# Splits of VectorE to GpSimd and ScalarE, five pair tiles ahead of the exchanged tiles and three behind, and x2 added per quarter

## The chip, the cores and the metric

The kernel runs on one core of a Trainium2 chip. The metric is the time of one execution on the device in microseconds (us). The core has five engines that run side by side, each with its own order of instructions: TensorE (PE, matrix products; PEld are its weight loads), VectorE (DVE), ScalarE (ACT), GpSimd (POOL) and SyncE (SP), which here issues the DMAs. They wait for each other with semaphores.

## What is computed

A decoder block with its normalisations behind (post-LN) on 16 sequences of 56 tokens, 128 features. The reference, cut to what matters:

```python
x = _layernorm(x + mix(x))            # convolution, gated phase sums over the sequence, output projection
x = _layernorm(x + attend(x, ctx))    # attention of 56 tokens on 1500 context rows per sequence
def ffn(tgt):                         # E=8 experts, F=512, top 2 of 8
    logits = tgt @ Wr.T + br
    top_v, top_i = top_k(logits, 2);  top_w = softmax(top_v)
    h = relu(einsum('bsd,efd->bsef', tgt, W1) + b1)
    o = einsum('bsef,edf->bsed', h, W2) + b2
    tgt2 = sum of the two chosen experts' rows of o, weighted with top_w
    return _layer_norm(tgt + tgt2) * gamma + beta
x = _layernorm(ffn(x))
```

## The kernel before

The 16 sequences are eight pairs of 112 tokens. The program is written out by hand for each engine (one function for each, in a block), with semaphores; nothing schedules it, so each engine's order is the order of the code. Mixing comes first, then eight turns of attention (one pair each, `attend_turn(i)` and `last_turn`), and behind them the expert layer and a tail.

**Expert layer.** The rows of seven pairs (784 tokens, two experts each) are exchanged: GpSimd scatters them by expert with indirect DMAs into `slots` (line 1861), SyncE loads them back as tiles of 112 rows (line 457 the eight fixed tiles, one for each expert; line 462 the 13 extra ones, whose expert is known at run time only). The eighth pair isn't exchanged: it is put through all eight experts in eight "pair tiles", and the sums weighted by `rw7` are gathered in `acc` (`pair_out`). `SEQUENCE` is the order: `HEAD` pair tiles, then tiles 0 to 20, then the other pair tiles. Each place n in it has a hidden product (`hidden(n)`, lines 782 and 784), ScalarE's `hidden_high(n)` (relu to fp16, line 1142), VectorE's `hidden_low(n)` (the rest in fp16, line 1681) and an output product (`outs(n)`, line 801). TensorE runs `hidden(n + 1)` before `outs(n)`. A tile is first turned by TensorE (`turn_tile`, line 761) two places ahead and copied out of PSUM to `xT` by VectorE (`turned_tile`, line 1673; tiles from 8 on by ScalarE, line 1148), for which `hidden` waits with `t_xv` and `t_xa`.

**Weights.** Each expert's weights (two halves, `which`) are split into a high and a low fp16 part: `split_high` on ScalarE (line 1038), `split_low` on GpSimd for experts 0 to 3 (line 1845; ScalarE scales the raw weights for it first, line 1036) and on VectorE for 4 to 7 (line 1697), between its other work at places 2 to 9. The extra tiles use copies of their expert's weights that VectorE makes (`staged`, lines 1689 and 1691). At places 1 to 3 VectorE also works out which expert each extra tile has: `count_extras` (lines 1505 to 1509), `expert_of_tile` (1514 to 1520) and `tile_map` (1525 to 1531).

**Tail.** GpSimd scatters each finished tile to `ret` (line 1948); when all have landed, SyncE loads the rows by quarters of the pairs into `got` (line 468, semaphores `g_ld`). TensorE adds `x2` and both returned rows of a quarter in PSUM with an identity matrix (`added`, line 824), VectorE takes mean and variance (`moments`), ScalarE the inverse deviation (lines 935 and 937), VectorE centres (line 1787), GpSimd scales (line 1958), TensorE adds the result to `x2b` (x2 plus beta, `with_beta`, `with_x2`), and a second normalisation follows (ScalarE's `final_norm`, VectorE's `vector_final`). The last pair goes the same way in `last_pair` without the exchange. SyncE stores the parts (line 474).

## Time and profile before

| | us |
|---|---|
| three runs | 194.76, 195.3, 197.42 (median 195.3) |
| profiled execution | 194.64 |
| its span | 192.8 |
| mean granted TensorE clock | 0.986 of full speed |
| TensorE busy | 175.0 (91%) |
| VectorE busy | 148.7 (77%) |
| ScalarE busy | 117.2 (61%) |
| GpSimd busy | 64.4 (33%) |

The span runs from the first instruction to the last; 1.8 us of the execution lie around it. Times in the trace are counted from the span's start. Busy shares are means over stages with different limits; they don't say what a stage waits for.

### The profile page before, as it was taken

The page shows a single profiled execution, that of the slowest core. Times are in us where ns is not written, and L with a number is a line of the kernel's source. Part 1 is how long each engine was busy: PE and PEld are TensorE (multiplying, and loading weights), DVE is VectorE, ACT ScalarE, POOL GpSimd, SP SyncE. Part 2 cuts the span into 40 slices and gives each one's busy share as a digit, 9 for nine tenths or more (in the row PEclk, how much of TensorE's full clock was granted, in tenths as well). Part 3 has the DMA queues.
Part 4 walks back from the last instruction along what each step waited for, and adds up shares of the span by engine and source line. Part 5 has one row for each costly group of instructions (what it writes and reads, how often), then busy time and mean ns, then how long its engine had stood idle before and what let it go on. Part 6 is the DMA issues. An engine that isn't in the chain of part 4 may idle for free.

```text
span 192.8 us, 4890 instructions
## 1 busy us (share of the span) xinstructions
PE 175.0 (91%) x1767; PEld 127.2 (66%) x1767; DVE 148.7 (77%) x383; ACT 117.2 (61%) x257; POOL 64.4 (33%) x83
## 2 busy tenths in 40 slices
PE   7999999978899899999999999797897999998950
PEld 6655454563453395674855797596897999998730
DVE  2669999989989988765767777567987889746782
ACT  2189979922646536687687874354564777642364
POOL 5000000000023400049588687630167555550130
PEclk9999999999999999999999999999999999999995
DMA  5999999994799439999767910114033201004102
GB/s 139 335 237 306 241 315 236 390 405 162 192 341 372 123 94 330 300 260 341 196 223 240 338 46 24 36 29 100 16 87 87 73 28 29 27 0 137 47 24 60
DMA packets 13355, 33.58 MB, mean 174 GB/s; under 512 B 2151, under 2 KB 5547, under 8 KB 13331
## 3 DMA queue, kind: packets, MB, share of 16 engines
q1 hardware_dynamic: 12212, 31.65, 54.6%
q0 software_dynamic: 1120, 1.62, 2.9%
q8 instruction: 14, 0.23, 0.5%
q14 instruction: 9, 0.07, 0.1%
HBM read 27.87 MB, written 5.80 MB: 175 GB/s over the span
## 4 chain that ended last, share of the span: by engine, by line
PE 68%; DVE 15%; issue 5%; ACT 4%; POOL 3%; DMA 2%; POOLq 0%; DVEq 0%; ACTq 0%
PE bank L496 9%; PE bank L801 8%; PE bank L551 8%; PE bank L784 7%; PE bank L576 7%; PE bank L506 5%; PE bank L563 4%; PE bank L515 3%; PE bank L824 3%; PE bank L484 3%; PE bank L782 3%; DVE ph L1549 3%; POOL slots L1861 2%; DVE home L1309 2%; DVE neg_max L1440 1%
## 5 line engine op out<-in xcount | busy, mean ns | idle before, releaser
L1948 POOL DMA_INDIRECT ret<-ctx_slot,ctxT_slot x21 | 20.2, 962 | 23.5 <-ACT ctx_slot L1155 13.5
L1142 ACT ACTIVATE ctx_slot<-bank 128x448 f16<-128x448 f32 x29 | 15.7, 543 | 17.0 <-PE bank L784 17.0
L1681 DVE SCALAR_TENSOR_TENSOR ctx_slot<-bank,ctx_slot 128x448 f16<-128x448 f32 x29 | 18.0, 622 | 9.2 <-ACT ctx_slot L1142 8.6
L551 PE MATMUL bank<-ctxT_slot,w_conv 97*64 97x500 f32 x96 | 21.8, 590 | 0.1
L1865 POOL TENSOR_TENSOR home<-home 128x896 f32<-128x896 f32 x1 | 2.1, 2081 | 53.4 <-ACT home L924 53.4
L496 PE MATMUL bank<-xpad,w_conv 128*128 128x448 f32 x48 | 18.2, 537 | 0.0
L1440 DVE TENSOR_REDUCE neg_max<-bank 120x1 f32<-120x1500 f32 x8 | 13.7, 1716 | 3.8 <-PE bank L551 3.8
L1309 DVE TENSOR_TENSOR_SCAN home<-reset,home 128x896 f32<-128x896 f32 x8 | 15.8, 2008 | 0.0
L1861 POOL DMA_INDIRECT slots<-mix,slot_i x14 | 13.4, 958 | 6.0 <-issue 3.8
L782 PE MATMUL bank<-half_sb,b_hl 128*128 128x112 f16 x64 | 12.8, 213 | 2.8 <-DVE home L1697 2.5
L576 PE MATMUL bank<-ctx_slot,ph 125*64 125x96 f32 x336 | 15.4, 248 | 0.0
L496 PEld LDWEIGHTS bank<-xpad,w_conv 128*128 128x128 f32 x48 | 9.1, 190 | 8.7 <-issue 8.7
L576 PEld LDWEIGHTS bank<-ctx_slot,ph 125*64 125x64 f32 x336 | 14.0, 133 | 1.2 <-issue 0.7
L801 PE MATMUL bank<-home,ctx_slot 128*112 128x128 f16 x192 | 13.7, 220 | 0.0
L484 PE MATMUL bank<-reset 128*128 128x224 f32 x44 | 12.4, 428 | 1.4 <-DVE reset L1208 1.4
L551 PEld LDWEIGHTS bank<-ctxT_slot,w_conv 97*64 97x64 f32 x96 | 6.0, 133 | 11.0 <-issue 10.7
L506 PE MATMUL bank<-home,w_blk 128*128 128x448 f32 x32 | 12.6, 542 | 0.0
L801 PEld LDWEIGHTS bank<-home,ctx_slot 128*112 128x112 f16 x192 | 12.1, 130 | 0.3
L784 PE MATMUL bank<-ctx_slot 128*128 128x112 f16 x156 | 11.7, 212 | 0.0
L484 PEld LDWEIGHTS bank<-reset 128*128 128x128 f32 x44 | 9.8, 238 | 2.2 <-DVE reset L1208 1.4
L801 PE MATMUL bank<-ctx_slot 128*112 128x128 f16 x156 | 11.0, 220 | 0.0
L515 PE MATMUL bank<-home,small_sb 128*128 128x448 f32 x24 | 9.9, 555 | 0.8 <-ACT home L924 0.8
(227 smaller groups left out, 433.2 us busy)
## 6 DMA issues: line engine op xcount, KB each, us to landing
ctx_slot<-ctx SPq DMA_DIRECT2D x16, 576.0 KB, 6.0
ctxT_slot<-ctx_T SPq DMA_DIRECT2D x16, 562.5 KB, 8.3
w_raw<-w SPq DMA_DIRECT2D x16, 256.0 KB, 7.0
slots<-w_raw SPq DMA_DIRECT2D x4, 796.2 KB, 24.9
ctxT_slot<-slots SPq DMA_DIRECT2D x21, 56.9 KB, 1.8
convw_sb<-conv_w SPq DMA_DIRECT2D x3, 256.0 KB, 5.6
ctxT_slot<-ret SPq DMA_DIRECT2D x3, 224.0 KB, 3.3
small_sb<-small SPq DMA_DIRECT2D x1, 522.5 KB, 8.2
```

What stands on the lines that cost most here:

```text
L484: mm = pe.matmul(bank[:, to, 0:HW // 2], reset[:, 0:D], reset[:, 0:HW // 2], start=True, stop=True)
L496: mm = pe.matmul(bank[:, Z[c, g], 0:HW], w_conv[:, g, k, :], xpad[:, HB * c:HB * (c + 1), k:k + L], start=(k == 0), stop=(k == TAPS - 1))
L506: mm = pe.matmul(bank[:, Y_BANK[c], 0:HW], w_blk[:, j, :], terms[:, j * HW:(j + 1) * HW], start=(j == 0), stop=(j == 2 * M - 1))
L551: mm = pe.matmul(bank[j * GAP:j * GAP + rows, n, 0:SN], qk_all[:, at:at + rows], ctxT_slot[:, s, j, n * SN:(n + 1) * SN], start=True, stop ...
L576: mm = pe.matmul(bank[j * GAP:j * GAP + rows, SUM_BANKS[i], 0:DC], expT_sb[i][:, c, j * GAP:j * GAP + rows], ctx_slot[0:KP, s, j, c, :], s ...
L782: pe.matmul(to, b1_hl[:, at], b[:, 0:cols], start=True, stop=False)
L784: mm = pe.matmul(to, w[:, 0, part, at], x[:, half, 0:cols], start=False, stop=(m == 2))
L801: mm = pe.matmul(to, h_[:, n % 3, f, 0:cols], w[:, 1, part, f * D:(f + 1) * D], start=False, stop=(h_ is hl and f == FC - 1))
L1309: return V.tensor_tensor_scan(sums[:, w], reset[:, 0:W2], terms[:, w], 0.0, ALU.mult, ALU.add)
L1681: V.scalar_tensor_tensor(hl[:, n % 3, :, 0:cols], bank[:, n % 3, 0:FC * TS].rearrange("p (f t) -> p f t", f=FC) [:, :, 0:cols], 0.0, hh[:, ...
L1861: G.indirect_dma_start(slots[:], bass.IndirectOffsetOnAxis(ap=slot_i[:, i, w:w + 1], axis=0), rows[:, i, w, :], None).then_inc(r_scat, 16)
L1948: G.indirect_dma_start(ret[:], bass.IndirectOffsetOnAxis(ap=xs_u[:, t, D + 1:D + 2], axis=0), out_st[:, t % OB, :], None, bounds_check=2 * ...
```

## The change

`HEAD` is 5: five pair tiles stand ahead of the exchanged tiles and three behind. `POOL_SPLITS` is 5: the low halves of expert 4 are split by GpSimd, right behind its last scatter, and ScalarE scales that expert's raw weights first. VectorE's own splits (experts 5 to 7) run at places 3 to 8. `XT` is 5: ScalarE copies the turned tiles from 5 on, VectorE only 0 to 4. The tile-map work of VectorE moves ahead by one place. ScalarE's high half `split_high(1, 4)` moves behind the last inverse deviation. On GpSimd a row subtraction takes the place of the third pause, and the last three additions of beta move ahead of the tiles' scatters. In the tail, `x2` is added quarter by quarter, directly ahead of each quarter's returned rows, and the order of the last pair's steps, of `with_beta`, `with_x2`, the inverse deviations and the stores is another.

```diff
-HEAD = 4
-POOL_SPLITS = 4
+HEAD = 5
+POOL_SPLITS = 5
+XT = 5
@@ sync
-            for n, w in enumerate((slice(XP, PAIRS), slice(0, 2), slice(2, 4), slice(4, 6), slice(6, XP))):
-                if 1 <= n < 4:
-                    sp_.wait_ge(f_out, n)
-                else:
-                    sp_.wait_ge(f_outv, 2 if n else 1)
+            for w, done, count in ((slice(0, 2), f_out, 1), (slice(2, 4), f_out, 2), (slice(XP, PAIRS), f_outv, 1),
+                                   (slice(6, XP), f_outv, 2), (slice(4, 6), f_out, 3)):
+                sp_.wait_ge(done, count)
                 sp_.dma_start(out[:, w, :], x1[:, w, :]).then_inc(s_store, 16)
@@ tensor: turn_tile, and the same in hidden
-                    pe.wait_ge(t_xv, min(t - 1, E))
-                if t - 2 >= E:
-                    pe.wait_ge(t_xa, t - 1 - E)
+                    pe.wait_ge(t_xv, min(t - 1, XT))
+                if t - 2 >= XT:
+                    pe.wait_ge(t_xa, t - 1 - XT)
@@ tensor: tail
             def returns(q):
                 w = slice(2 * q, min(2 * q + 2, XP))
+                added(SUM_AT[q], x2[:, w, :], start=True)
                 pe.wait_ge(g_ld[q], 16)
...
+            returns(0)
+            returns(1)
             pe.wait_ge(t_hl, len(SEQUENCE))
-            pe.wait_ge(t_acc, E)
             pe.wait_ge(m_x2b, PAIRS)
-            for q in range(4):
-                added(SUM_AT[q], x2[:, 2 * q:min(2 * q + 2, XP), :], start=True)
-            returns(0)
             with_beta(0)
-            returns(1)
-            with_beta(1)
             returns(2)
             with_x2(0)
+            pe.wait_ge(t_acc, E)
+            with_beta(1)
+            returns(3)
+            with_x2(1)
             with_beta(2)
-            returns(3)
             with_beta(3)
-            with_x2(1)
             with_x2(2)
             with_x2(3)
@@ scalar
-            split_high(1, RAW - 1)
...
             attended_inv_std(PAIRS - 1)
+            split_high(1, RAW - 1)
...
-                if HEAD <= n + 2 < HEAD + TILES and SEQUENCE[n + 2][1] >= E:
+                if HEAD <= n + 2 < HEAD + TILES and SEQUENCE[n + 2][1] >= XT:
                     turned_tile(SEQUENCE[n + 2][1])
...
             final_inv_std(0, False)
+            final_inv_std(1, False)
             final_inv_std(0, True)
-            final_inv_std(1, False)
             final_inv_std(2, False)
             final_inv_std(1, True)
             final_inv_std(3, False)
             final_norm(0)
+            final_inv_std(2, True)
             final_inv_std(4, False)
-            final_inv_std(2, True)
@@ vector: expert layer
-                if HEAD - 2 <= n < HEAD + E - 2:
+                if HEAD - 2 <= n < HEAD + XT - 2:
                     turned_tile(n + 2 - HEAD)
...
                 if n == 1:
-                    scanned = count_extras()
+                    summed_tiles = expert_of_tile(count_extras())
                 if n == 2:
-                    summed_tiles = expert_of_tile(scanned)
-                if n == 3:
                     tile_map(summed_tiles)
-                if 2 <= n < 4:
-                    split_low(n - 2, RAW - 1)
-                if 4 <= n < 10:
-                    split_low(n % 2, RAW + (n - 4) // 2)
+                if 3 <= n < 9:
+                    split_low((n - 3) % 2, RAW + (n - 3) // 2)
@@ vector: tail (last_pair is cut in last_centred and last_summed, returned in returned and centred)
-            last_pair()
+            centred_last = last_centred()
             returned(0)
-            vector_final(0)
+            centred(0)
+            last_summed(centred_last)
             returned(1)
+            centred(1)
             summed(0)
             returned(2)
+            centred(2)
             final_bias(0)
             summed(1)
             returned(3)
+            centred(3)
+            summed(2)
             final_bias(1)
-            summed(2)
+            vector_final(0)
             summed(3)
@@ gpsimd
             pause(1)
             scatter(5, 0)
-            pause(2)
+            low_rows(6)
             scatter(5, 1)
-            low_rows(6)
             second_weights(4)
             scatter(6, 0)
             scatter(6, 1)
+            split_low(0, 4)
+            split_low(1, 4)
+            for i in range(PAIRS - 3, PAIRS):
+                plus_beta(i)
...
-                if 2 <= t < 5:
-                    plus_beta(PAIRS - 5 + t)
```

What stands in a row on the engines, at three places. First VectorE at places 1 to 3 of the expert layer, before, from the scan of the counts (line 1509) on; line 1673 is the copy of a turned tile, 1681 `hidden_low`, 1708 the pair's sum, 1697 a weight split:

```order
L1509 SCALAR_TENSOR_TENSOR counts<-ones,counts 1x8
L1673 COPY ctx_slot<-bank 128x224
L1681 SCALAR_TENSOR_TENSOR ctx_slot<-bank,ctx_slot 128x448
L1708 SCALAR_TENSOR_TENSOR xtok<-bank,rw,xtok 112x128
L1514 TENSOR_TENSOR ge<-counts,small_sb 1x104
L1517 TENSOR_REDUCE mapf<-ge 1x13
L1518 TENSOR_TENSOR ge_n<-ge,counts 1x104
L1520 TENSOR_REDUCE mapf<-ge_n 1x13
L1697 SCALAR_TENSOR_TENSOR home<-w_raw,home 128x512
L1673 COPY ctx_slot<-bank 128x224
```

And now (the lines are up to three lower: 1506, 1670, 1678, 1705, 1694):

```order
L1506 SCALAR_TENSOR_TENSOR counts<-ones,counts 1x8
L1511 TENSOR_TENSOR ge<-counts,small_sb 1x104
L1514 TENSOR_REDUCE mapf<-ge 1x13
L1515 TENSOR_TENSOR ge_n<-ge,counts 1x104
L1517 TENSOR_REDUCE mapf<-ge_n 1x13
L1678 SCALAR_TENSOR_TENSOR ctx_slot<-bank,ctx_slot 128x448
L1705 SCALAR_TENSOR_TENSOR xtok<-bank,rw,xtok 112x128
L1522 TENSOR_SCALAR map_e<-mapf 1x13
L1523 SCALAR_TENSOR_TENSOR mapf<-small_sb,mapf 1x13
L1525 SCALAR_TENSOR_TENSOR mapf<-mapf 1x13
L1528 TENSOR_SCALAR map_r<-mapf 1x13
L1670 COPY ctx_slot<-bank 128x224
```

The comparisons and the map now stand in one place each earlier, no split stands between, and the first turned copy comes behind the whole map, where before it came behind the scan alone.

GpSimd at the end of the exchange, before (line 1884 is a pause, 1861 a scatter of rows, 1836 and 1852 prepare rows, 1948 scatters a finished tile, 1841 adds beta):

```order
L1884 MEMSET xpad 128x300
L1861 DMA slots<-mix,slot_i 6384x130
L1836 TENSOR_TENSOR mix<-rows_late,mix 112x2x128
L1852 TENSOR_TENSOR mix<-mix,tsm 112x1
L1861 DMA slots<-mix,slot_i 6384x130 x2
L1948 DMA ret<-ctx_slot,ctxT_slot 1568x128 x3
L1841 TENSOR_TENSOR rows_late<-rows_late,small_sb 112x128
```

And now (1841 prepares rows, 1850 splits weights, 1846 adds beta):

```order
L1866 DMA slots<-mix,slot_i 6384x130
L1841 TENSOR_TENSOR mix<-rows_late,mix 112x2x128
L1866 DMA slots<-mix,slot_i 6384x130
L1857 TENSOR_TENSOR mix<-mix,tsm 112x1
L1866 DMA slots<-mix,slot_i 6384x130 x2
L1850 TENSOR_TENSOR home<-w_raw,home 128x512 x2
L1846 TENSOR_TENSOR rows_late<-rows_late,small_sb 112x128 x3
L1956 DMA ret<-ctx_slot,ctxT_slot 1568x128 x21
```

The subtraction stands where the pause was, and two splits and the three additions stand in a row between the last scatter and the first finished tile.

TensorE behind its last output product, before (`rows_late` holds x2 and x2 plus beta, `ctxT_slot` the returned rows, `xtok` the scaled ones):

```order
L801 MATMUL bank<-home,ctx_slot 112x128 x12
L824 MATMUL bank<-rows_late,small_sb 112x256 x3
L824 MATMUL bank<-rows_late,small_sb 112x128
L824 MATMUL bank<-ctxT_slot,small_sb 112x256 x2
L824 MATMUL bank<-rows_late,small_sb 112x256
L824 MATMUL bank<-ctxT_slot,small_sb 112x256 x2
L824 MATMUL bank<-rows_late,small_sb 112x256
L824 MATMUL bank<-ctxT_slot,small_sb 112x256 x2
```

And now:

```order
L800 MATMUL bank<-home,ctx_slot 112x128 x12
L823 MATMUL bank<-rows_late,small_sb 112x256
L823 MATMUL bank<-ctxT_slot,small_sb 112x256 x2
L823 MATMUL bank<-rows_late,small_sb 112x256
L823 MATMUL bank<-ctxT_slot,small_sb 112x256 x2
L823 MATMUL bank<-rows_late,small_sb 112x256 x2
L823 MATMUL bank<-ctxT_slot,small_sb 112x256 x2
L823 MATMUL bank<-xtok,small_sb 112x256
```

One addition of x2 instead of four stands ahead of the first returned rows.

## Rows read from the trace of the kernel before

**Rows 1.** The page's part 4: shares of the chain that ended last.
```profile
PE 68%; DVE 15%; issue 5%; ACT 4%; POOL 3%; DMA 2%; POOLq 0%; DVEq 0%; ACTq 0%
```

**Rows 2.** TensorE's timeline: start, length (us), instruction, idle time before and its releaser.
```profile
128.22 0.21 PE L782 MATMUL bank<-half_sb,b_hl 128*128 128x112 f16 x1
...
130.94 0.27 PE L761 MATMUL bank<-half_sb,ctxT_slot 112*128 112x112 f16 x2 [1.04 <-DMA ctxT_slot<-slots]
...
135.28 0.21 PE L782 MATMUL bank<-half_sb,b_hl 128*128 128x112 f16 x1 [0.83 <-DVE home L1697]
...
138.92 0.26 PE L761 MATMUL bank<-half_sb,ctxT_slot 112*128 112x112 f16 x2
139.02 0.21 PE L782 MATMUL bank<-half_sb,b_hl 128*128 128x112 f16 x1
...
140.54 0.26 PE L761 MATMUL bank<-half_sb,ctxT_slot 112*128 112x112 f16 x2
...
146.94 0.22 PE L782 MATMUL bank<-half_sb,b_hl 128*128 128x112 f16 x1 [1.29 <-DVE home L1697]
```

**Rows 3.** VectorE's timeline of the same stretch.
```profile
130.95 0.16 DVE L1509 TENSOR_TENSOR_SCAN counts<-ones,counts 1x8 f32<-1x8 f32 x1
...
133.41 0.24 DVE L1514 TENSOR_TENSOR ge<-counts,small_sb 1x104 f32<-1x104 f32 x1
...
134.32 0.67 DVE L1697 SCALAR_TENSOR_TENSOR home<-w_raw,home 128x512 f16<-128x512 f32 x1
134.92 0.26 DVE L1673 COPY ctx_slot<-bank 128x224 f16<-128x224 f16 x1
...
145.98 0.90 DVE L1697 SCALAR_TENSOR_TENSOR home<-w_raw,home 128x512 f16<-128x512 f32 x1
```

**Rows 4.** TensorE's timeline where the tail begins.
```profile
177.56 1.74 PE L824 MATMUL bank<-rows_late,small_sb 112*112 112x256 f32 x8 [0.49 <-issue]
179.14 1.03 PE L824 MATMUL bank<-ctxT_slot,small_sb 112*112 112x256 f32 x4
```

**Rows 5.** Line 468, time to landing: first load alone, then first two.
```profile
DMA to landing us min/median/max: 3.3/3.3/3.3
...
DMA to landing us min/median/max: 3.3/3.8/4.2
```

**Rows 6.** VectorE's timeline in the tail, and the stores' line 474.
```profile
180.21 0.49 DVE L1753 BATCH_NORM_STATS2 stat<-bank 112x6 f32<-112x128 f32 x2 [0.64 <-PE bank L824]
...
187.53 0.16 DVE L1799 SCALAR_TENSOR_TENSOR nmr<-mv,rstd 112x2 f32<-112x2 f32 x1 [0.63 <-ACT rstd L937]
...
189.59 0.41 DVE L1805 TENSOR_SCALAR x<-bank,mv,rstd 112x128 f32<-112x128 f32 x1 [0.45 <-ACT rstd L937]
...
L474 SPq DMA_DIRECT2D out<-x x5: 316/322/427, 181.9 to 190.6; - x5
```

**Rows 7.** GpSimd's timeline: one pause and the last scatter.
```profile
122.00 0.36 POOL L1884 MEMSET xpad<- 128x300 f32 x1
...
126.40 0.94 POOL L1861 DMA_INDIRECT slots<-mix,slot_i  x1 [0.30 <-issue]
```

**Rows 8.** ScalarE's timeline: last pair's exponential, and copy of `x7`.
```profile
108.29 1.51 ACT L968 ACTIVATE convw_sb<-bank,neg_max 120x1500 f32<-120x1500 f32 x1
...
124.69 0.25 ACT L1133 CAST turned_late<-bank 128x112 f16<-128x112 f32 x1 [1.37 <-PE bank L600]
```

**Rows 9.** Groups of GpSimd's instructions: count, busy us, mean ns, idle before.
```profile
L1845 POOL TENSOR_TENSOR home<-w_raw,home 128x512 f16<-128x512 f32 x8 | 9.2, 1161 | 2.5 <-ACT home L1038 2.4
```

**Rows 10.** VectorE's line 1570 twice, and GpSimd beside the second.
```profile
113.11 0.35 DVE L1570 TENSOR_SCALAR rows_late<-res,attend_mv,attend_rstd 112x128 f32<-112x128 f32 x1
...
123.71 0.57 DVE L1570 TENSOR_SCALAR rows_late<-res,attend_mv,attend_rstd 112x128 f32<-112x128 f32 x1
...
123.51 0.68 POOL L1836 TENSOR_TENSOR mix<-rows_late,mix 112x256 f16<-112x256 f32 x1
```

**Rows 11.** Stretch, length, busy us by engine, granted TensorE clock, DMA.
```profile
188.00:189.00 1.00, 0.44 (x2) 0.12 (x1) 0.84 (x6) 0.92 (x4) 0.00 (x0) 0.50 0.00 0
```

More of the change, by code:

```diff
@@ L772, in hidden @@
                 else:
-                    pe.wait_ge(t_xv, min(k + 1, E))
-                    if k >= E:
-                        pe.wait_ge(t_xa, k + 1 - E)
+                    pe.wait_ge(t_xv, min(k + 1, XT))
+                    if k >= XT:
+                        pe.wait_ge(t_xa, k + 1 - XT)
                     x = xT[:, k % 3]
```

13 lines of the change are left out of this document (8 added, 5 removed).

## Prediction

> **What bounds the kernel now.** I read the page first: TensorE carries two thirds of the chain that ended last [rows 1]. So TensorE's own order is followed, and what counts is each place where it stops. The change touches nothing of weight ahead of the expert layer, so I read TensorE's timeline from 125 us on, and looked at what released it after each stop [rows 2]. In the steady part one tile starts 1.62 us after the last (138.92 to 140.54). 0.10 of that is the turning of the tile after next, so a pair step is 1.52. Against that rhythm it stands still in three places. (a) It waits for tile 0's rows and restarts at 130.94. `hidden(2)` started at 128.22, so it could have gone on at 129.74: 1.20 lost. (b) It restarts at 135.28 after 0.83 idle (and once more, for less, at the next tile): it wants the turned tile in `xT`, which is VectorE's `turned_tile`, queued on VectorE behind the tile-map arithmetic and the weight splits (the trace names the split at line 1697). (c) It restarts at 146.94 after 1.29 us idle, when VectorE has split the last half of expert 7. Rows 3 show VectorE there: the counts' scan at 130.95, the comparisons from 133.41 to 134.32, a split of 0.67, the turned copy only at 134.92, and the last split at 145.98, 0.90 long.
>
> Behind the expert layer the tail begins: TensorE adds `x2` into four banks from 177.56, and only from 179.14 the returned rows [rows 4]. The first quarter of these was loaded from 174.05 and landed 3.3 us later, at 177.35; the second was issued at 174.4 and took 4.2 [rows 5]. So in the tail the load is not late; TensorE's pair tiles and the eight `x2` matmuls are. From there VectorE sets the pace: 180.21 to 189.59, with the last store issued at 190.6 [rows 6].
>
> **The change, part by part.** Times are of the profiled execution, 192.8 us of span and 194.64 us in all; the 1.8 around the span I take as unchanged. The median of the three runs, 195.3, is 0.7 above it.
>
> *A fifth pair tile in front.* At 129.74 TensorE now has a pair step to do before it turns tile 0, so it turns it at 129.74 + 1.52 = 131.26. Tile 0 had landed by 130.94, so stop (a) is covered with 0.3 to spare; moving a row subtraction in the place of the second pause in front of the last scatters brings the last scatter, before at 126.40, forward by about one memset of 0.36 [rows 7]. Hidden layer 4 (pair 4) then starts at 131.36.
>
> *Splits of expert 4 to GpSimd.* VectorE loses two splits (2 x 0.60 from start to start). ScalarE gets two scalings of about 0.6. One lies ahead of the exponential of the last pair, which began at 108.29, right behind the split; it ends 0.6 later, near 110.6, and TensorE wants it at 111.5: cost nothing, cover 0.9. The other pair of ScalarE instructions (about 1.2) moves into the wait between the last inverse deviation and the copy at 124.69 [rows 8]: ScalarE was idle 1.37 us there, so it fits, with 0.2 to spare. I take 0, and 0.1 as the bound. GpSimd splits for 1.16 each [rows 9]: after a last scatter that ends near 127.0, until 129.4, then the three additions of beta until 130.8. TensorE wants expert 4 at 131.36: covered by 2 us.
>
> *VectorE's new order* (lengths from start to start in the timeline of rows 3). The scan starts at 130.58 as part of three small steps and ends at 131.15. The comparisons follow at once, 0.91, to 132.06. `hidden_low(3)` takes 0.53, the pair sum 0.26, the map 0.53, and the turned copy of tile 0 starts at 133.38 and ends at 133.65. So hidden layer 5 (tile 0) starts at 133.75, where TensorE could have begun at 132.98. A wait of 0.8 is left of the old (a) and (b). Tile 1 starts at 135.37 without a wait; tile 2 at 137.08 (0.1 late, behind one split of 0.60); from tile 3 (138.70) VectorE needs 0.54 + 0.60 + 0.27 = 1.41 a step and keeps up. Tile 7 then starts at 137.08 + 5 x 1.62 = 145.18, and expert 7 was split three steps earlier: (c) is gone. Before, tile 7 started at 146.94. **Tiles run 1.76 earlier**, though a pair more lies ahead of them.
>
> *What GpSimd's work does to VectorE.* Here the trace has few rows, in both directions. VectorE's line 1570 took 0.57 us at 123.71, while GpSimd's subtraction of 0.68 ran, and 0.35 at 113.11 beside a scatter; a split took 0.90 beside GpSimd's work against 0.67 alone [rows 3, 7, 10]. So an overlap cost 0 to 0.22. Between 127.0 and 130.8 four small VectorE operations ahead of `hidden_low(1)` (lines 1468, 1663, 1664, 1667) now have GpSimd's splits beside them. 4 x 0.22 = 0.88, less the 0.45 that VectorE then idled before 129.78: 0.4. Bounds 0 and, if each waits for a whole GpSimd instruction, 1.2 (below). I take 0.4, the size that the rows show. **Tiles run 1.36 earlier.**
>
> A rule bears on this. The Trainium skill (SBUF — State Buffer, section "Who interferes with whom") says that a VectorE instruction in a two-port mode contends with GpSimd for one port pair, and that the second to issue blocks until the first has finished. By that rule the charge would be the 1.2 of the rival below. The trace agrees in part: the 0.57 us instruction ended 0.09 after GpSimd's.
>
> *Three pairs behind instead of four.* TensorE finishes its last pair at 177.07 - 1.36 - 1.52 = 174.19. The last tile's scatter, and so the load of the returned rows, moves only by the 1.36: first quarter landed at 177.35 - 1.36 = 175.99. So of the 2.9 that TensorE wins, 1.5 turns into a new wait for the rows. The `x2` matmuls of the first quarter lie in this wait; those of the others go between the quarters, 0.45 each (3.5 of that size took from 177.56 to 179.14).
>
> *The tail.* The returned rows are added from 176.0 instead of 179.14: 3.1 earlier. The next waits: quarter 2 has landed at 178.6 - 1.36 = 177.2 when TensorE wants it at 177.3; TensorE has the four sums ready at about +1.0, +2.3, +4.0 and +5.5 from 176.0, VectorE takes them at +1.1, +3.3, +5.3 and +7.4. VectorE is the pace. Between its first and second quarter now stands the last pair's second step (0.83), and its last normalisation (0.25) goes into a wait near the end, where VectorE had idled 0.63 and 0.45 [rows 6]. Followed instruction by instruction, the span from VectorE's first quarter to the last store's issue was 190.6 - 180.21 = 10.4 and becomes about 10.65; the last store is twice as large, 0.1. So 0.35 is given back.
>
> Sum: -3.15 + 0.35 = -2.8. Profiled time 194.64 - 2.8 = 191.9. Against the median of 195.3 that is 1.7%.
>
> **The rivals.**
> 1. *The splits cost VectorE nothing.* For it: line 1570 beside a scatter kept its 0.35. Then tiles run 1.76 earlier: 191.5.
> 2. *Each locking VectorE operation waits for GpSimd's whole instruction*, by the rule above. The operation at 127.62 waits to 128.2, the one at 128.00 to 129.4, the next two behind additions to 130.2; `hidden_low(1)` starts at 130.3 instead of 128.54. VectorE could run 0.45 + about 0.2 into its gaps, so tile 0 comes 1.1 to 1.2 later: 191.5 + 1.15 = 192.6. For it: the 0.57. Against: the same line at 113.11, which no scatter held up.
> 3. *TensorE's clock falls in the new wait.* Between 174.2 and 176.0 TensorE has only 0.4 us of work. The row for it: after the gaps that TensorE has near the end, the granted clock was 0.50 in 188 to 189 [rows 11], that is 1.2 instead of 2.4 GHz. If it falls at 176 and stays there, every tail matmul doubles: 17.5 additions of 256 columns, 7.9 us, become 15.8, the sums and not VectorE set the pace, and the last store is issued 4 us later: 191.9 + 4.0 = 195.9, slower than before. It decides only if low clock lasts through the tail; for one or two us of it VectorE's slack (1 to 2 us from the second quarter on) hides most, 192.5. Against it: TensorE also stood still in (a) and (c), 1.0 and 1.3 us, and the mean granted clock of the whole span is 0.986, which leaves room for little more than the end.
> 4. *It does nothing*: VectorE is as late as before, because three more steps' work still stands ahead of tile 0's copy, and the waits only change places. (a) to (c) would have to come back as 2.8 us of new waits: 194.6. The added wait for the rows is certain; the rest isn't in the rows.
>
> **How the numbers follow.** Chances: the forecast (191.4 to 192.2) 0.40, the first rival 0.2, the second 0.25, the third 0.08 (nearly all of it the short form), the fourth or something of its size 0.07. The likeliest gives 191.9. Low end: the first rival, less the 1.0 us that VectorE waits in the tail [rows 6], if all of it is filled, 190.5; high end: the second with the short form of the third, and the 0.7 of the median over the profile, 194.3. Outside I leave 0.2. Two per cent, about what a measurement of this kernel can tell from no change, is 3.9 us, so faster means under 191.4: the better half of the first rival and a little of the forecast, 0.2. Slower means over 199.2: 0.02. The rest, 0.78.
>
> **What the changed profile would show.** Right: no stop of TensorE at tile 0's load nor ahead of tile 7, one of 0.5 to 1.2 ahead of tile 0's hidden layer, released by VectorE's turned copy; tile 7 near 145.5; the last pair done near 174.2, then some 1.5 us in which TensorE waits for the returned rows; VectorE nearly without a gap from 177 to 185. Wrong: VectorE's small operations near 128 us with 0.5 us or more each (second rival); 256-column additions of 0.9 instead of 0.45 in the tail (third); TensorE's first hidden layer later than 125.39, if ScalarE's moved split is in the way.

## The result, and the profile after

Twenty executions of each kernel: the changed one takes 194.03 us (median), the one before 194.79. The ratio of the undisturbed executions (those that ran some per cent longer are left out, here and in every ratio below) is 0.9944 [0.9917, 0.9970], a gain of about 1.1 us, or 0.76 between the two medians, where 2.8 were forecast. The profiled execution of the changed kernel took 195.49 us, span 193.7; it is one of the longer ones (the shortest took 192.84), and the account below says why.

The chain that ended last, first its shares:

```profile
PE 51%; DVE 16%; issue 12%; POOL 9%; DMA 6%; ACT 5%; SPq 0%; ACTq 0%; DVEq 0%; POOLq 0%
```

TensorE had 68% of it [rows 1]. What it lost went to GpSimd, to issue and to DMA, and most of that is no new wait: the end now waits for the returned rows, so the chain is followed back through the last tile scatter and from there through the scatters before it (0.89 POOL and 0.73 issue for each tile, which is TensorE's own rhythm of 1.62). Where time was lost is read from the timelines. The one where expert 4's splits now lie, rows of VectorE and GpSimd (start, length in us, instruction):

```profile
127.41 2.27 POOL L1850 TENSOR_TENSOR home<-w_raw,home 128x512 f16<-128x512 f32 x2
...
127.90 2.54 DVE L1465 TENSOR_TENSOR chosen<-small_sb,topi 112x16 f32<-112x16 f32 x1
...
129.64 1.13 POOL L1846 TENSOR_TENSOR rows_late<-rows_late,small_sb 112x128 f32<-112x128 f32 x3
...
131.11 0.62 DVE L1678 SCALAR_TENSOR_TENSOR ctx_slot<-bank,ctx_slot 128x448 f16<-128x448 f32 x1
...
135.52 0.25 DVE L1670 COPY ctx_slot<-bank 128x224 f16<-128x224 f16 x1
```

One VectorE instruction of 16 columns lasts 2.54 us. It began half a microsecond after GpSimd's first split and ended when two splits and two of three additions were through (the additions are 0.4 each: 129.64 + 0.8 = 130.44), ahead of the third. Behind it on VectorE stand the pair's weights and `hidden_low(1)`, at 131.11. TensorE's timeline shows who pays:

```profile
131.79 0.43 PE L800 MATMUL bank<-home,ctx_slot 128*112 128x128 f16 x4 [1.84 <-DVE ctx_slot L1678]
133.57 0.26 PE L760 MATMUL bank<-half_sb,ctxT_slot 112*128 112x112 f16 x2
...
135.88 0.21 PE L781 MATMUL bank<-half_sb,b_hl 128*128 128x112 f16 x1 [0.43 <-issue]
...
147.19 0.26 PE L760 MATMUL bank<-half_sb,ctxT_slot 112*128 112x112 f16 x2
```

A stop of 1.84 in the second output layer, where there was none. The stops (a), (b) and (c) [rows 2] (at tile 0's load, ahead of the first turned tile, ahead of tile 7) are gone but for 0.43. From tile 0's hidden layer (135.88) the steps are 1.62, with no stop at tile 7, whose hidden layer follows the turning at 147.19 by 0.10. So tiles run 0.35 later than before (146.94), not 1.36 earlier. The first hidden layer stood at 125.39 before and is at 125.67 here. Where the tail begins (GpSimd's last tile scatter, SyncE's loads, TensorE):

```profile
172.33 0.94 POOL L1956 DMA_INDIRECT ret<-ctx_slot,ctxT_slot  x1 [0.31 <-issue]
175.27 1.72 SPq L469 DMA_DIRECT2D ctxT_slot<-ret  x4
175.75 0.64 PE L823 MATMUL bank<-rows_late,small_sb 112*112 112x256 f32 x2
178.10 1.12 PE L823 MATMUL bank<-ctxT_slot,small_sb 112*112 112x256 f32 x4 [1.72 <-DMA ctxT_slot<-ret]
...
179.61 1.91 PE L823 MATMUL bank<-ctxT_slot,small_sb 112*112 112x256 f32 x4
```

The new wait for the returned rows is there, 1.72. The returned rows are added from 178.10, 1.04 earlier than before [rows 4], and then four such additions take 1.91 instead of 1.03. The stretches say what that is (length, busy us by engine, granted TensorE clock, DMA):

```profile
178.00:179.00 1.00, 0.90 (x4) 0.77 (x5) 0.00 (x0) 0.00 (x0) 0.00 (x0) 1.00 0.90 245
179.00:180.00 1.00, 1.00 (x5) 0.72 (x4) 0.71 (x4) 0.00 (x0) 0.00 (x0) 0.68 0.23 81
180.00:181.00 1.00, 1.00 (x4) 0.72 (x3) 0.93 (x5) 0.50 (x2) 0.06 (x1) 0.50 0.00 0
...
183.00:184.00 1.00, 1.00 (x7) 0.79 (x6) 0.00 (x0) 0.00 (x0) 0.61 (x1) 1.00 0.00 0
```

From 179.4 to 182.8 the granted clock is 0.50, that is 1.2 GHz. VectorE, which was to be the pace, now waits for the sums (it had waited 0.64 at the first quarter [rows 6]):

```profile
184.40 0.50 DVE L1746 BATCH_NORM_STATS2 stat<-bank 112x6 f32<-112x128 f32 x2 [1.42 <-PE bank L823]
```

The span was forecast at 190.0 and is 193.7. Stretch by stretch, this execution minus the forecast: start of the expert layer +0.28; from there to tile 0's hidden layer +1.45 (10.21 against 134.15 - 125.39 = 8.76); tile steps 0.0 (36.45 against 36.48); last scatter to SyncE's load +0.88 (2.94 against 2.06 before); load to landing -0.5 (2.8 against 3.3); returned rows to the end +1.6 (15.6 against 14.0). Sum 3.7. Three of these are large (+1.45, +0.88 and +1.6), and each has its experiments.

### The profile page after: what moved, and what is told of

Its sections match the earlier page's. It is cut to its first block, busy times and chain, and to the rows that moved or that the text cites. A ratio compares the mean times of both kernels' runs of the same rounds, so it can differ in the third digit from the quotient of the medians.

```text
span 193.7 us, 4891 instructions
## 1 busy us (share of the span) xinstructions
PE 175.8 (91%) x1767; PEld 127.6 (66%) x1767; DVE 149.0 (77%) x378; ACT 119.1 (61%) x262; POOL 65.5 (34%) x84
## 3 DMA queue, kind: packets, MB, share of 16 engines
q0 software_dynamic: 1120, 1.62, 2.8%
## 4 chain that ended last, share of the span: by engine, by line
PE 51%; DVE 16%; issue 12%; POOL 9%; DMA 6%; ACT 5%; SPq 0%; ACTq 0%; DVEq 0%; POOLq 0%
PE bank L495 9%; POOL ret L1956 9%; PE bank L550 8%; PE bank L575 7%; PE bank L505 5%; PE bank L562 4%; PE bank L514 3%; PE bank L823 3%; DMA xpad<-x_T 3%; DVE ph L1546 3%; DVE home L1306 2%; PE bank L783 2%; DMA ret<-ctx_slot,ctxT_slot 2%; DMA ctxT_slot<-ret 1%; DVE neg_max L1437 1%
## 5 line engine op out<-in xcount | busy, mean ns | idle before, releaser
L800 PE MATMUL bank<-home,ctx_slot 128*112 128x128 f16 x192 | 13.9, 220 | 1.8 <-DVE ctx_slot L1678 1.8
L575 PE MATMUL bank<-ctx_slot,ph 125*64 125x96 f32 (+1 forms) x336 | 15.4, 248 | 0.0
L575 PEld LDWEIGHTS bank<-ctx_slot,ph 125*64 125x64 f32 (+1 forms) x336 | 14.0, 133 | 1.2 <-issue 0.7
L483 PE MATMUL bank<-reset 128*128 128x224 f32 x44 | 11.8, 410 | 1.4 <-DVE reset L1205 1.4
L1850 POOL TENSOR_TENSOR home<-w_raw,home 128x512 f16<-128x512 f32 x10 | 11.5, 1162 | 2.5 <-ACT home L1036 2.4
L933 ACT ACTIVATE lnv<-mv,cst 112x1 f32<-112x1 f32 (+2 forms) x14 | 4.1, 291 | 12.4 <-DVE mv L1749 8.3
```

The lines of the kernel that those rows point to most:

```text
L575: mm = pe.matmul(bank[j * GAP:j * GAP + rows, SUM_BANKS[i], 0:DC], expT_sb[i][:, c, j * GAP:j * GAP + rows], ctx_slot[0:KP, s, j, c, :], s ...
L800: mm = pe.matmul(to, h_[:, n % 3, f, 0:cols], w[:, 1, part, f * D:(f + 1) * D], start=False, stop=(h_ is hl and f == FC - 1))
```

## The experiments

Each ran beside the kernel before; ratios are to that kernel on the same chip. On three of the chips every kernel, the kernel before too, has a median of 201 to 207 us, with TensorE's tile steps near 2 us on the average instead of 1.62 and wide intervals. In each profile from these chips ScalarE stands still for about 2 us at least once behind tile 0, released by what the profile only calls "remote", and TensorE waits behind it or behind VectorE's weight copies; in the profiles from the other chips neither occurs. Why is open. The runs a0, a1, e6 to e11, e15 and e16 come from these chips, so there I lean on intervals within a profile. The changed kernel itself gave 1.0007 [0.9943, 1.0070] and 0.9941 [0.9896, 0.9985] on two of them, which shows how far such ratios can be trusted.

**1. GpSimd beside VectorE.** Three edits of the changed kernel: wait first (e1), give VectorE's `hidden_low(1)` the place ahead of the choice (e2), put gaps between GpSimd's instructions (e3).

```diff
@@ e1, GpSimd
+            pool.wait_ge(m_rw7, 1)
             split_low(0, 4)
             split_low(1, 4)
@@ e2, VectorE
             hidden_low(0)
+            hidden_low(1)
             choose(XP, PAIRS)
... (and it is left out at its old place)
@@ e3, GpSimd
             split_low(0, 4)
+            pool.wait_ge(m_wl, 9)
             split_low(1, 4)
+            pool.wait_ge(m_wl, 10)
             for i in range(PAIRS - 3, PAIRS):
                 plus_beta(i)
+                pool.wait_ge(m_x2b, i + 1)
```

> GpSimd starts its two splits of expert 4 and the three additions only when VectorE has made the last pair's weights (one wait added on GpSimd; all else as in the changed kernel). Port theory: the comparison at line 1465, which took 2.54 us with GpSimd's splits beside it, is back at 0.17; hidden_low(1) starts near 128.8 instead of 131.1; TensorE's 1.84 us stop in outs(1) is gone; GpSimd's splits end near 131.4, just when TensorE wants them, so tile 0's hidden layer starts at 134.0 to 134.6 instead of 135.9. Time 1.2 to 1.8 us under the changed kernel, about 192.3. Rival (the comparison waited for its input or for something of VectorE's own, not for GpSimd's port): it stays long wherever the splits are, no gain. Second rival: the wait only moves, since the splits now come late for hidden layer 4 and lie beside other VectorE operations with two SBUF operands: under 0.5 us of gain.

> Only VectorE's order differs from the changed kernel: hidden_low(1) stands ahead of the last pair's comparison instead of behind it; GpSimd is untouched. Port theory in the form 'only operations with two SBUF operands wait': hidden_low(1), which reads PSUM and one SBUF operand, runs at about 128.6 beside GpSimd's split in its usual 0.6 us, and the comparison behind it is again held until about 130.4, so it takes about 1.3 us; TensorE stops later and for less, time 0.5 to 1.0 us under the changed kernel. If any VectorE operation is held while GpSimd works, hidden_low(1) is long too (over 1.5 us) and nothing is won. If the comparison was waiting for its input, it is short now.

> As the changed kernel, but GpSimd waits for its own last result between its two splits and its additions, so that they no longer follow without a break. If the port is handed over at the end of each GpSimd instruction, and VectorE lost only because GpSimd's next one stood ready, the comparison now ends with the first split: about 0.8 us instead of 2.54, and the next operations are held once more by the second split; hidden_low(1) starts near 130.0 instead of 131.1; 0.5 to 1 us gained. If VectorE waits as long as GpSimd has work at all, the comparison still takes about 2.5 us and nothing changes.

e1: 193.84 us, ratio 0.9939 [0.9909, 0.9969]. Its timeline, rows of VectorE, GpSimd and, at tile 0, TensorE:

```profile
127.62 0.16 DVE L1465 TENSOR_TENSOR chosen<-small_sb,topi 112x16 f32<-112x16 f32 x1
...
128.54 0.62 DVE L1678 SCALAR_TENSOR_TENSOR ctx_slot<-bank,ctx_slot 128x448 f16<-128x448 f32 x1
...
128.71 2.28 POOL L1850 TENSOR_TENSOR home<-w_raw,home 128x512 f16<-128x512 f32 x2 [1.60 <-DVE rw L1664]
...
130.58 0.42 DVE L1502 TENSOR_SCALAR counts<-counts 1x8 f32<-1x8 f32 x1
131.04 0.34 DVE L1504 TENSOR_SCALAR counts<-counts 1x8 f32<-1x8 f32 x1
...
134.56 0.21 PE L781 MATMUL bank<-half_sb,b_hl 128*128 128x112 f16 x1 [0.50 <-issue]
```

The choice is back at 0.16 and `hidden_low(1)` at 128.54, exactly as before the change. Tile 0's hidden layer comes 1.04 earlier, from the same start, than in the changed kernel (9.17 against 10.21). What is left over 133.75 is now four counting operations, held 0.8 together, since GpSimd's work moved beside them. The cause is shown; in time, e1's interval overlaps that of the changed kernel, so the runs don't show the 1 us, let alone the 1.2 to 1.8 that were expected.

e2: 194.17 us, 0.9971 [0.9944, 0.9997]. In its timeline both VectorE instructions begin while GpSimd splits:

```profile
128.06 2.29 POOL L1851 TENSOR_TENSOR home<-w_raw,home 128x512 f16<-128x512 f32 x2
...
129.31 0.63 DVE L1678 SCALAR_TENSOR_TENSOR ctx_slot<-bank,ctx_slot 128x448 f16<-128x448 f32 x1 [0.65 <-ACT ctx_slot L1140]
...
129.85 1.26 DVE L1465 TENSOR_TENSOR chosen<-small_sb,topi 112x16 f32<-112x16 f32 x1
```

The large one, which reads a bank of PSUM and one SBUF operand, keeps its 0.63 in the midst of the splits; the small one, with two SBUF operands, is held to 131.1. It is the larger one that isn't held; that the operands decide is what these rows suggest, and no run tried it apart (in e3 an operation on `chosen` and a scale, line 1660, was held as well, while a small one that reads PSUM, line 1496, kept its 0.15 just ahead of it). Tile 0's hidden layer comes 0.34 earlier (9.87 from the first one, against 10.21); the 0.5 to 1.0 expected of the time doesn't show in the ratio.

e3: 194.58 us, 0.9956 [0.9925, 0.9987]. The same rows of its timeline:

```profile
128.99 2.41 POOL L1850 TENSOR_TENSOR home<-w_raw,home 128x512 f16<-128x512 f32 x2
...
129.50 0.71 DVE L1465 TENSOR_TENSOR chosen<-small_sb,topi 112x16 f32<-112x16 f32 x1
...
130.25 1.18 DVE L1660 TENSOR_SCALAR rw<-chosen,tsm 112x8 f32<-112x8 f32 x1
```

With a gap behind the first split the choice gets through at its end (0.71), and the next VectorE operation with its input in SBUF is held by the second split (1.18). Tile 0's hidden layer is 9.32 behind the first one, 0.89 earlier than in the changed kernel. So in the changed kernel it was the unbroken row of GpSimd instructions that held one VectorE instruction 2.4 us: it didn't get its turn between the first four of them. It did ahead of the fifth, and in e2 as well (131.1, where the third addition begins); why there, no run shows.

> Expert 4's two weight splits are given back to VectorE (0.60 each, beside the second and third pair step); all else stays. Theory (GpSimd's chain of splits and additions holds VectorE's small operations 2.4 us and is what the forecast missed): VectorE's choice goes back to 0.2 to 0.9 us (three additions of 0.40 remain beside it), hidden layer 1 comes 1.5 us or more earlier, tile 0's hidden layer is 0.5 to 1.2 us earlier than in the changed kernel, less up to 1.2 for the two splits on VectorE: time 193.2 to 193.8. Rival (where the splits are made doesn't matter, since the two splits cost VectorE the same 1.2 us they saved): 194.0, as the changed kernel. Rival (GpSimd's help is worth its price): 194.5 or more.

e6 makes expert 4's splits on VectorE again. Ratio 1.0042 [1.0000, 1.0085]. The choice is at 0.16, as expected, but I had put the second split behind the comparisons: TensorE waits for it, once, longer than any hold cost. Its TensorE timeline:

```profile
137.64 0.28 PE L781 MATMUL bank<-half_sb,b_hl 128*128 128x112 f16 x1 [3.24 <-DVE home L1694]
```

So e6 says nothing on the price of handing the splits over: its own delay hides it.

**2. The new wait and TensorE's clock.** e4 puts dummy matrix work into the wait, e8 the other three quarters' additions of `x2`.

```diff
@@ e4, TensorE, in returns(q), behind the addition of x2
+                if q == 0:
+                    keep_warm(4, 7)
@@ e8, TensorE (returns without its addition, and without the wait for t_hl behind returns(1))
+            for q in range(4):
+                if q == 2:
+                    pe.wait_ge(t_hl, len(SEQUENCE))
+                added(SUM_AT[q], x2[:, 2 * q:min(2 * q + 2, XP), :], start=True)
             returns(0)
```

> As the changed kernel, with four matmuls on unused data (about 0.4 us each) in TensorE's wait for the returned rows. Clock theory: the 1.9 us instead of 1.03 for four 256-column additions at 179.6, and VectorE's 1.4 us stop at 184.4, come from TensorE's clock falling to half because of that wait; kept busy, the granted clock stays 1.00 until 188, VectorE has no stop over 0.6 us in the tail, and the profiled time is 1.2 to 1.5 us lower than that of the changed kernel (195.5), about 194.0; the median less, since not each execution loses the clock: 0.3 to 1.0. Rival (the tail is late because the returned rows land late): the median doesn't move, and the additions take 0.45 each already in most executions.

> All four quarters' additions of x2 stand ahead of the first returned rows, as before the change, so that 1.3 us more of TensorE's work lies in the new wait, and 1.3 us less behind it. Theory (the wait is for the load, whose landing is set by the last tile's scatter, and the work in it is free): the wait shrinks from 1.7 to about 0.4 us, the first sum is as early, the clock stays at 2.4 GHz, and the time is 0.3 to 1.0 us under the changed kernel, 193.1 to 193.7. Rival (VectorE is the pace at the end and the clock falls anyway): 193.9 to 194.1.

e4: 193.49 us, 0.9929 [0.9907, 0.9951]. e8: 1.0011 [0.9963, 1.0058], on a chip where the changed kernel had 1.0007. TensorE in the tail of e4:

```profile
175.70 1.68 PE L483 MATMUL bank<-reset 128*128 128x224 f32 x8
178.01 1.12 PE L823 MATMUL bank<-ctxT_slot,small_sb 112*112 112x256 f32 x4 [0.64 <-DMA ctxT_slot<-ret]
178.97 0.59 PE L823 MATMUL bank<-rows_late,small_sb 112*112 112x256 f32 x2
179.40 1.03 PE L823 MATMUL bank<-ctxT_slot,small_sb 112*112 112x256 f32 x4
```

The clock stays at 2.4 GHz here. From the first returned rows to the end of the span it is 13.9 us in e4, 13.85 in e8, and 13.8 to 14.0 in e1, e6, e7, e10, e11, e12, e14 and a0, whose clocks stayed up over this stretch too (14.8 and 14.3 in e2 and e3, where TensorE waited once more, 0.61 and 0.20, for the second quarter). It is 15.6 in the changed kernel's first profile and 16.9 in a later one (a1): 1.7 and 3.1 more, which is half of the 3.4 and 6.2 us that the low clock lasted there. e8's earlier additions shorten nothing else: its 13.85 is that of the others.

Whether the clock falls is less certain than one profile suggests. The longest stop of TensorE behind the last tile, in a1, a0 and e7, where in the last two ScalarE is waited for and not the rows:

```profile
188.38 2.05 PE L823 MATMUL bank<-ctxT_slot,small_sb 112*112 112x256 f32 x4 [1.94 <-DMA ctxT_slot<-ret]
```

```profile
184.38 1.33 PE L800 MATMUL bank<-home,ctx_slot 128*112 128x128 f16 x12 [2.45 <-ACT ctx_slot L1140]
```

```profile
182.13 1.09 PE L800 MATMUL bank<-home,ctx_slot 128*112 128x128 f16 x12 [2.42 <-ACT ctx_slot L1140]
```

Seven profiles have such a stop of 1.70 us or more. In five the granted clock fell to 0.50: the changed kernel's first (1.72) and a1 (1.94, already in the wait, at 187.8), and a0 (2.45), e11 (1.70) and e16 (2.40), where it was back at 1.00 before the rows were added. In two it stayed: e1 (1.78) and e7 (2.42). In the other twelve, with stops of 1.22 or less, it stayed for at least 7 us from the first returned rows on. So all three profiles of the changed kernel have the fall, two of them at the wait for the rows; but e1 has the same wait without it, and one profile each of e4 and e8 can't prove that the filling kept the clock up. The mean clocks of the changed kernel's sixteen executions in the ratio show that it differs from one to the next: the five with 0.994 or more took 192.84 to 193.56 us, the three with 0.981 or less 194.1 to 195.67. Where in them the clock was low they don't tell.

**3. The load that goes out late.** SyncE's first load waits for the scatters. From the last scatter's start it is 2.06 us before, 2.94 here, 2.45 to 3.28 in e1 to e4. The DMA view has a queue of instruction transfers; over the 4 us from the last scatter's start (40 slices of 0.1 us, GB/s), first before, then here:

```profile
GB/s 0 0 0 4 1 0 0 0 0 0 0 0 0 0 0 3 2 0 0 0 0 0 0 0 0 164 0 0 0 0 123 102 143 164 123 246 369 369 266 164
```

```profile
GB/s 0 0 0 4 1 0 0 0 0 164 0 0 0 0 0 84 2 0 0 1 0 0 0 0 0 0 0 0 0 0 0 0 0 0 0 0 0 0 41 61
```

The small marks at 0.3 and 1.5 us are the scatter; 164 in a slice is an instruction transfer of 16 KB. Before, it came at 2.5 us, when the load was out; now it comes at 0.9, and one of 8 KB at 1.5. With a pair less behind the tiles, TensorE's program reaches that place 1.5 us sooner. To tell the effect of the transfer from that of the pair tiles, e12 (changed kernel) and e13 (kernel before) lengthen TensorE's program near its beginning:

```diff
-            keep_warm(7).then_inc(s_warm, 1)
+            for _ in range(45):
+                mm = pe.matmul(bank[:, O_BANK[0], 0:120], reset[:, 0:64].bitcast(F16), reset[:, 0:60].bitcast(F16),
+                               start=True, stop=True)
+            mm.then_inc(s_warm, 1)
```

> The changed kernel, whose first warming of TensorE (14 matrix instructions that compute nothing) is cut into 45 smaller ones of about the same length together, so that all later instructions of TensorE lie 62 places further on in its program. Nothing else differs. Theory (the load of the returned rows is issued late because a transfer of TensorE's instructions runs between the last tile's scatter and its completion; in six profiles with the one inside that time the load follows the last scatter's start by 2.45 to 3.28 us, in five with none inside by 2.06 or 2.07): the transfer moves 1.6 us forward, ahead of the last scatter's start, and the load follows that by 2.1 to 2.5 us instead of 2.94; the wait for the returned rows shrinks to under 1.3 us and the clock stays up: 0.5 to 1.5 us less than the changed kernel. Rival (the lag comes from having three pair tiles behind the last tile tile, not from the transfer): the lag stays near 3 us and the time as the changed kernel.

> The kernel before with the same cut of the first warming: its transfer of TensorE's instructions, which came 2.5 us after the last scatter's start, comes 1.6 us earlier, into the scatter's time. Theory: the load of the returned rows follows the last scatter's start by 2.9 to 3.3 us instead of 2.06, though four pair tiles stand behind; the rows land 0.9 to 1.2 us later, at the time at which TensorE wants them or a little after: 0 to 0.5 us slower than the kernel before. Rival: the lag stays 2.06.

e12: 193.39 us, 0.9935 [0.9897, 0.9972]. e13: 194.47 us, 0.9983 [0.9956, 1.0010]. The same DMA row for e12 and for e13, each from its last scatter's start, and between them the scatter and the load in e13's timeline:

```profile
GB/s 0 0 0 4 1 0 0 0 0 0 0 0 82 0 0 2 3 0 0 0 0 0 0 0 0 0 0 0 0 0 0 0 0 0 82 102 102 102 82 143
```

```profile
172.20 0.94 POOL L1951 DMA_INDIRECT ret<-ctx_slot,ctxT_slot  x1 [0.30 <-issue]
...
176.14 1.73 SPq L468 DMA_DIRECT2D ctxT_slot<-ret  x4
```

```profile
GB/s 0 0 0 4 1 0 0 0 0 0 0 0 0 0 0 2 2 164 0 0 0 0 0 0 0 0 0 0 0 0 0 0 82 0 0 0 0 0 0 0
```

e12's last scatter starts at 172.03 and its load goes out at 174.54: the large transfer has moved ahead of the scatter (171.5), and the load follows by 2.51. VectorE's and GpSimd's programs are those of the changed kernel, so it isn't something that they do beside the scatter. In e13 the transfer moved from 2.5 to 1.7, less than I had reckoned, and the load follows by 3.94 instead of 2.06, with four pairs behind. It cost the kernel before next to nothing, as expected: TensorE was busy with the additions of `x2` until 179.36, against 179.14 [rows 4]. All profiles fit: no transfer between 0.4 and 1.8 us behind the scatter's start, 2.06 or 2.07 (six profiles: before, a0, e6, e7, e11, e16); only the 8 KB one, 2.50 to 2.61 (e3, e12, e14); the 16 KB one, 2.94 to 3.94 (eight). e2, with 8 KB at 1.2 and 16 KB at 1.9, had 2.45, and e15, with 16 KB at 1.9 alone, 2.07. The pair tiles alone do nothing: a0 is the changed kernel, three behind, with 2.07. In time e12 shows little, 0.9935 where 0.5 to 1.5 us less than the changed kernel's 0.9944 was expected, and its wait for the rows is 1.10.

**4. The fifth pair itself, and all edits together.** e7 and e11 are the changed kernel with `HEAD = 4`. e9 is e1 and e8; e10 adds the three additions of beta back among the tile scatters; e14 adds the cut warming to e10; e15 is e14 with `HEAD = 4`; a0, a1 and e16 are the changed kernel and e14 once more.

```diff
@@ e10 and e14, GpSimd, over e9
             split_low(1, 4)
-            for i in range(PAIRS - 3, PAIRS):
-                plus_beta(i)
...
+                if 2 <= t < 5:
+                    plus_beta(PAIRS - 5 + t)
```

> Four pair tiles in front and four behind, as before the change; all the rest of the change stays (the new splits, VectorE's order, the order at the end). Theory (the fifth pair in front only moves a pair step from behind the tiles to the wait for tile 0; what it wins is what TensorE stood still for at tile 0, 0.5 to 1.2 us, and behind the tiles the wait for the returned rows eats the rest): TensorE stops at tile 0 for 0.5 us more, the wait of 1.7 us at the end shrinks to under 0.5, the clock stays at 2.4 GHz through the end, and the time is within 0.5 us of the changed kernel, 193.5 to 194.5. Rival (the fifth pair is where the gain is): 195 or more. Rival (it costs, through the clock): under 193.3.

> GpSimd's two splits and three additions of beta start only when VectorE has made the last pair's weights, and all four quarters' additions of x2 stand ahead of the first returned rows. Theory (the splits beside VectorE's small operations cost about 1.1 us, the idle wait for the returned rows and the clock that falls behind it some tenths to 1.7): 0.988 to 0.992 of the kernel before, 192.4 to 193.2 where that takes 194.8. Rival (VectorE, and not TensorE, sets the pace from the returned rows on, and the additions of beta still hold VectorE's counting operations): 0.993 to 0.995.

> As the kernel with both edits, and the three additions of beta go back among the tile scatters, so that GpSimd has nothing beside VectorE's counting operations but the second split. Theory: tile 0's hidden layer is 0.3 to 0.6 us earlier than with the additions in front, 0.985 to 0.990 of the kernel before. Rival (the additions are short, and elsewhere among the scatters they delay a scatter or a copy of VectorE by as much): the same time as with both edits.

> All together: GpSimd's splits after the last pair's weights, the additions of beta among the tile scatters, the four additions of x2 ahead of the returned rows, and the cut warming. Theory: each removes one of the three losses (VectorE held beside GpSimd, the idle wait with its falling clock, the transfer beside the last scatter): 0.982 to 0.988 of the kernel before. Rival (the losses hide one another): 0.988 to 0.992, as without the cut warming.

> The version with all four edits, but with four pair tiles in front and four behind. Theory (once VectorE is not held, the fifth pair in front covers the load of tile 0 and VectorE's work ahead of its turned copy, and is worth at least 1 us, of which the wait for the returned rows gives back some): TensorE stops 1.0 us or more ahead of tile 0, and the time is 0.5 to 1.5 us more than with five. Rival (behind the tiles a pair is worth as much, since the rows are waited for anyway): the same time within 0.3 us.

e7: 0.9928 [0.9867, 0.9989]; e11, the same program on another chip: 1.0012 [0.9958, 1.0066]. e9: 1.0113 [1.0029, 1.0197], a miss: its profile has the half clock in the first hidden layers of the expert layer (four at 0.37 us instead of 0.20) and a lag of 3.26. Why the clock was low there I can't say, and the 2.3% between e9 and e10 on one chip are more than three moved additions explain (8.64 in e14 against 9.17 in e1: 0.5 us). e10: 0.9881 [0.9836, 0.9926]. e14: 191.92 us, 0.9870 [0.9811, 0.9929]; again as e16: 0.9890 [0.9813, 0.9968]. TensorE in e14, at tile 0 and in the tail:

```profile
134.06 0.21 PE L784 MATMUL bank<-half_sb,b_hl 128*128 128x112 f16 x1 [0.49 <-issue]
...
174.11 1.72 PE L826 MATMUL bank<-rows_late,small_sb 112*112 112x256 f32 x8
176.14 1.99 PE L826 MATMUL bank<-ctxT_slot,small_sb 112*112 112x256 f32 x8 [0.31 <-DMA ctxT_slot<-ret]
```

With all three losses taken away, the forecast's figures appear: from the first hidden layer (125.42) to the last scatter (170.70) 45.28 us against 45.24 forecast, returned rows added at 176.14 against 176.0, a span of 190.0 against 190.0. Part of that is luck: the load goes out 2.61 behind the last scatter, not 2.06, and lands 0.5 sooner than forecast. The gain is 1.1 to 1.3%, against 0.6% of the changed kernel; the intervals still touch (0.9929 and 0.9917).

e15: 0.9835 [0.9739, 0.9930], beside e16 on its chip. It has the stop ahead of tile 0 that was expected:

```profile
135.20 0.21 PE L784 MATMUL bank<-half_sb,b_hl 128*128 128x112 f16 x1 [1.07 <-issue]
```

But from the first hidden layer (127.39) to this one are 7.81 us; in e16, with five pairs in front, 9.11 (126.14 to 135.25). A fifth pair step of 1.52 makes the tiles 1.30 later: it covers 0.2 us of the stop. VectorE's share of that step (0.53 + 0.26) stands ahead of the turned copy too; what makes up the other 0.5 isn't worked out. Theory and expected slowdown of e15 fell. In time four against five pairs in front is 0.9835 against 0.9890, 0.9928 against 1.0007 (e7, a0) and 1.0012 against 0.9941 (e11, a1), with wide intervals: no worth of the fifth can be measured. But all six runs are from the chips where ScalarE stands still, and in none of the six but a1 did TensorE wait for the returned rows; in e16 it stood 2.40 us for ScalarE behind the tiles, with half the clock behind that. Where the steps are 1.62, four in front wasn't run. An estimate from e14 with the 1.3 of these two: with four, the rows would land 1.3 earlier, at 174.8, while TensorE, with 0.2 more of stops, would be ready for them at 176.05 (in e14 at 175.83, with a wait of 0.31), against 176.14 now. By that the 1.5 us won behind the tiles would be gone again, since the rows come 1.3 us later, and the fifth pair would be worth nothing. No run shows it.

## Why the prediction was wrong

- **The step that failed** is "What GpSimd's work does to VectorE": a charge of 0.4, bounds 0 and 1.2. Measured are 10.21 - 8.36 = 1.85 from the first hidden layer to tile 0's, against the 8.36 without contention; e14, with the splits out of the way, has 8.64. The upper bound was wrong too, and with it the second rival's time: it let each VectorE operation wait for one whole GpSimd instruction. One waited for four. I had read the size off [rows 10], where a single subtraction stood beside, and the charge of 4 x 0.22 has no term for a row of instructions without a gap.
- The Trainium skill (SBUF — State Buffer, section "Who interferes with whom") says that the port pair is an exclusive lock between VectorE and GpSimd; the second rival was that rule. The trace agrees in kind: the 16-column operation was held 2.4 us, the one that reads PSUM and a single SBUF operand not (0.63 in e2). It goes further in size: held until the fourth of GpSimd's instructions had finished, not the first. I took the rows' 0.22 over the rule, and gave it 0.25.
- **The new wait** was forecast at 1.5 and is 1.72, in the right place. The third rival (the clock falls in it) was given 0.08; of the changed kernel's three profiles it happened in the two that have this wait. The forecast's tail had nothing for it. Its short form (0.6 more for one or two us, since VectorE's slack hides most) was sized too low: 3.4 us of low clock cost 1.7 and 6.2 cost 3.1, so the slack hid nothing. The argument against it, stops (a) and (c) with 1.0 and 1.3 us, rested on shorter stops.
- **The load**: I took "2.06 behind the last scatter" as fixed. It moved by +0.88 through a transfer of instructions that the change brought beside the scatter, and the landing by -0.5. No row that I read shows this queue.
- **Stops (a), (b), (c)**: right. All three are gone; e14 puts tile 0's hidden layer at 134.06 where 133.75 was worked out. ScalarE's moved work was free, GpSimd's splits were in time for expert 4, as forecast: TensorE's first hidden layer is at 125.39 in e1 and e12, as before.
- **The fifth pair** "covers stop (a)": right, but the step it costs lies on the path of the tiles, and the estimate above leaves nothing of its gain. The forecast's sum holds all the same, since it had the later tiles and the wait in it.
- **The tail**: 14.0 forecast from the first returned rows; 13.8 to 14.0 where the clock stays.
- **The range**: 194.03 lies in 190.5 to 194.3, but by luck. The upper end is said to be the second rival (192.6) with the third's short form (0.6) and 0.7 for the median, which add up to 193.9. And the base was off: the 1.7% compares a forecast made from the profiled 194.64 with the median 195.3 of three executions, and twenty have 194.79. The 2.8 us are 1.4%.

What the executions hold: of the 2.8 us, e14 has 2.5 by its ratio and 3.0 by its median, the changed kernel 1.1 and 0.8. The difference is the three losses together. How it divides among them in an ordinary execution stays open, since each single repair (e1, e4, e12: 0.9939, 0.9929, 0.9935) has an interval that overlaps that of the changed kernel.

## What to carry to other kernels

Before work is handed to GpSimd, look at what VectorE does beside it, and charge a VectorE operation with two SBUF operands more than one of the GpSimd instructions that it falls into, if they follow without a gap (here four of five); put such a row behind the last small operation on which another engine waits, or break it up. Work moved from behind a stage to the front of it delays that stage and all that it releases: the gain is only what it covers there (here 0.2 of 1.5 us in e15 and e16). If a shortened stretch of TensorE leaves it waiting for a load, look at both its clock behind the wait and the instruction transfers around the DMA that is waited for.

## What the runs showed of the hardware

- One VectorE instruction of 112x16 elements took 2.54 us beside two GpSimd instructions of 1.16 and two of 0.40 without a gap between them; with a gap behind the first it took 0.71. It got through ahead of a third of 0.40. A 128x448 one with its input in PSUM and one operand in SBUF kept 0.63.
- An instruction transfer of 16 KB on TensorE's behalf, 0.8 to 1.7 us after the start of a scatter whose own data take two slices of 0.1 us, puts off the load that waits for the scatter: it goes out 2.94 to 3.94 us behind the scatter's start instead of 2.06; with one of 8 KB alone at 1.2 us, 2.50 to 2.61.
- Inserting 31 matrix instructions at the beginning of the program brings such a transfer, some 170 us further on, 0.8 (e13) and 1.4 us (e12) closer to the program's start, against the last scatter.
- Behind stops of TensorE of 1.70 to 2.45 us near the end the granted clock fell from 1.00 to 0.50 in five profiles and stayed in two (1.78, 2.42). In the changed kernel's first profile it fell 1.2 us after TensorE had resumed, in a1 0.6 us before. Low clock of 3.4 and 6.2 us over the tail's sums cost 1.7 and 3.1 us.
